# GpSimd's long subtractions split into two or four instructions each, in a two-layer decoder kernel

## The reference

```python
# layer 0: power attention with gates, 16 query heads on 8 key heads of 128
q, k, v = x @ Wq, x @ Wk, x @ Wv;  log_g = log_sigmoid(6.906768 + x @ Wg)
a = where(causal, (q k^T / sqrt(128)) ** 2 * exp(logG_t - logG_s), 0)
y = (a @ v / (sum(a) + 1e-6)) @ Wc + bc
# layer 0: causal attention on the context, 16 heads of 32, chunks of 256
# layer 0: experts: a router over 128, top 4, turned by amplitudes into 8 weights
#          for 8 gated bases of width 256, and two shared ones
...
# layer 1: multi-query attention with a memory, quantized cross attention,
#          a router over 8 small experts, top 2
```

## Time and profile before

| | |
|---|---|
| median of 3 runs | 2374.72 us (2372.3 to 2374.88) |
| profiled execution | 2378.91 us |
| its span | 2377.1 us |
| mean granted TensorE clock | 0.95 of full |
| PE busy | 2108.7 us, 89% |
| DVE busy | 1305.2 us, 55% |
| ACT busy | 1060.7 us, 45% |
| POOL busy | 796.7 us, 34%, 679 instructions |

### The profile page before, as it was taken

How to read it: one execution, slowest core, us unless ns; L and a number is a source line. 1 busy time by engine, 2 the same in 40 slices (tenths; PEclk the granted TensorE clock), 3 DMA queues, 4 the chain that set the end, 5 groups by cost and what they waited for, 6 DMA issues and landing times.

```text
span 2377.1 us, 37602 instructions
## 1 busy us (share of the span) xinstructions
PE 2108.7 (89%) x13655; PEld 1672.7 (70%) x13669; DVE 1305.2 (55%) x3333; ACT 1060.7 (45%) x2367; POOL 796.7 (34%) x679
## 2 busy tenths in 40 slices
PE   7899999898999978999999999968999778888764
PEld 6788888687878856877777888755555367666442
DVE  2554545544465456545456411356777676777555
ACT  3332332444444424445533312145666557777632
POOL 1743533333343222134431134254445231322100
PEclk9899999899999988999999999979999889999886
DMA  3311112011012012011110011033324210000001
GB/s 132 126 36 63 45 35 73 18 58 47 27 49 62 19 36 71 25 52 48 33 50 18 18 54 74 7 52 54 61 49 62 87 41 28 15 19 6 1 10 71
DMA packets 57878, 109.03 MB, mean 46 GB/s; under 512 B 7136, under 2 KB 35040, under 8 KB 54112
## 3 DMA queue, kind: packets, MB, share of 16 engines
q1 hardware_dynamic: 57696, 106.63, 15.4%
HBM read 86.10 MB, written 4.26 MB: 38 GB/s over the span
## 4 chain that ended last, share of the span: by engine, by line
PE 39%; DVE 10%; issue 7%; ACT 4%; POOL 2%; SPq 1%; DMA 1%; ACTq 0%; DVEq 0%; POOLq 0%
PE PS L1289 17%; PE PS L1880 3%; PE PS L1784 3%; PE PS L1305 2%; DVE st L191 2%; ACT xP L2545 2%; DVE aM L2020 1%; PE PS L1848 1%; PE PS L953 1%; PE PS L1868 1%; PE PS L965 1%; DVE PS L2667 1%; PE PS L1835 1%; ACT xN L240 1%; PE PS L1891 1%
## 5 line engine op out<-in xcount | busy, mean ns | idle before, releaser
L1289 PE MATMUL PS<-WH,bXH 128*128 128x512 f32 x640 | 258.7, 404 | 0.0
L1289 PE MATMUL PS<-WH,bXL 128*128 128x512 f32 x640 | 250.3, 391 | 0.0
L1289 PE MATMUL PS<-WL,bXH 128*128 128x512 f32 x640 | 250.2, 391 | 0.0
L2020 DVE TENSOR_REDUCE aM<-PS 128x4 f32<-128x1024 f32 x128 | 153.8, 1221 | 55.2 <-PE PS L1848 54.0
L384 PE MATMUL PS<-aXH,QKH 128*128 128x512 f32 x384 | 158.9, 414 | 14.6 <-ACT sq L597 8.4
L1586 POOL TENSOR_TENSOR mixed<-mixed,s 128x256 f32<-128x256 f32 x112 | 82.4, 739 | 245.5 <-DVE s L1487 245.3
L1590 POOL TENSOR_TENSOR WL<-sg,WH 128x2048 fp32r<-128x2048 f32 x20 | 92.1, 4604 | 186.5 <-ACT WH L1405 186.5
L384 PE MATMUL PS<-aXH,QKL 128*128 128x512 f32 x384 | 154.3, 402 | 0.0
L384 PE MATMUL PS<-aXL,QKH 128*128 128x512 f32 x384 | 154.0, 401 | 0.0
L1959 ACT ACTIVATE aPT<-PS 128x1024 f32<-128x1024 f32 x128 | 128.6, 1024 | 49.8 <-PE PS L1868 49.0
L684 DVE TENSOR_TENSOR qkL<-PS,qkH 128x512 fp32r<-128x512 f32 x96 | 65.9, 690 | 141.1 <-ACT qkH L561 141.0
(11 more groups left out here) (395 smaller groups left out, 6038.1 us busy)
## 6 DMA issues: line engine op xcount, KB each, us to landing
sg<-in_gu SPq DMA_DIRECT2D x16, 1024.0 KB, 4.8
gQK<-in_Wqk SPq DMA_DIRECT2D x16, 768.0 KB, 6.2
gC<-in_Wc SPq DMA_DIRECT2D x16, 512.0 KB, 7.0
lgB<-gate_sums SPq DMA_DIRECT2D x32, 256.0 KB, 4.6
aqs<-aQH SPq DMA_DIRECT2D x64, 128.0 KB, 4.1
xN<-in_xT SPq DMA_DIRECT2D x4, 1024.0 KB, 11.1
xN<-in_x SPq DMA_DIRECT2D x4, 1024.0 KB, 7.7
cst<-in_cT SPq DMA_DIRECT2D x8, 512.0 KB, 4.0
```

The source lines that it names most:

```text
L1289: mm = e.matmul(PS[:, b, :], x[:, kc, c:c + 128], y[:, kc, :], start=kc == 0 and n == 0, stop=kc == KC - 1 and n == 2)
L2020: e.tensor_reduce(M[j % 2][:, :, :].rearrange("x q (h c) -> x h q c", h=2)[:, :, :, i], PS[:, b:b + 2, :].rearrange("p h (q k) -> p h q k" ...
```

## The change

Six subtractions on POOL are each written as two or four instructions on the slices of their middle axis. The semaphore is raised by the last of them, and all waits stay where they were. The subtractions before the first step of `attention0` (L741, L744) are not changed. No other engine's sequence is changed.

```diff
-                    e.tensor_tensor(QKL[:, :, :], gQK[:, :, :], QKH[:, :, :].bitcast(F32),
-                                    ALU.subtract).then_inc(qk_lo.sem, 1)
+                    for kc in range(KC):
+                        last = e.tensor_tensor(QKL[:, kc, :], gQK[:, kc, :], QKH[:, kc, :].bitcast(F32), ALU.subtract)
+                    last.then_inc(qk_lo.sem, 1)
...
-                e.tensor_tensor(CL[:, :, :], gC[:, :, :], CH[:, :, :].bitcast(F32),
-                                ALU.subtract).then_inc(c_lo.sem, 1)
+                for h in (0, 1):
+                    last = e.tensor_tensor(CL[:, h, :], gC[:, h, :], CH[:, h, :].bitcast(F32), ALU.subtract)
+                last.then_inc(c_lo.sem, 1)
...
-                e.tensor_tensor(VL[:, :, 0:256], gV[:, :, 0:256], VH[:, :, 0:256].bitcast(F32),
-                                ALU.subtract).then_inc(v_lo.sem, 1)
+                for kc in range(KC):
+                    last = e.tensor_tensor(VL[:, kc, 0:256], gV[:, kc, 0:256], VH[:, kc, 0:256].bitcast(F32), ALU.subtract)
+                last.then_inc(v_lo.sem, 1)
...
-                    e.tensor_tensor(KL[:, c, :], cst[:, c, :], KH[:, c, :].bitcast(F32),
-                                    ALU.subtract).then_inc(k_lo.sem, 1)
+                    for k in (2 * i, 2 * i + 1):
+                        last_ = e.tensor_tensor(KL[:, k, :], cst[:, k, :], KH[:, k, :].bitcast(F32), ALU.subtract)
+                    last_.then_inc(k_lo.sem, 1)
...
-                e.tensor_tensor(WL[w % 2][:, :, :], sg[:, :, :], WH[w % 2][:, :, :].bitcast(F32),
-                                ALU.subtract).then_inc(w_lo.sem, 1)
+                for kc in range(KC):
+                    last_ = e.tensor_tensor(WL[w % 2][:, kc, :], sg[:, kc, :], WH[w % 2][:, kc, :].bitcast(F32), ALU.subtract)
+                last_.then_inc(w_lo.sem, 1)
...
-                e.tensor_tensor(DL[:, c:c + 2, :], dst[:, :, :], DH[:, c:c + 2, :].bitcast(F32),
-                                ALU.subtract).then_inc(d_lo.sem, 1)
+                for a in (0, 1):
+                    last_ = e.tensor_tensor(DL[:, c + a, :], dst[:, a, :], DH[:, c + a, :].bitcast(F32), ALU.subtract)
+                last_.then_inc(d_lo.sem, 1)
```

## The result

| | before | after |
|---|---|---|
| median | 2373.45 us (22 runs, 2366.63 to 2378.62) | 2369.71 us (22 runs, 2365.01 to 2376.52) |
| ratio | | 0.9984, 95% interval 0.9977 to 0.9992 |
| span of the profiled execution | 2377.1 us | 2368.8 us |
| POOL busy | 796.7 us in 679 | 822.0 us in 836 |

The changed kernel is 3.7 us faster (1.9 to 5.5 by the interval), less than the 0.2% that I called no change. I had forecast 2372.5 us and a gain of 2.25; 1.3 us of the distance to 2369.71 is the median of before, which was 2374.72 in the three runs that I had and is 2373.45 in 22. The two spans differ by 8.3 us, more than the medians.

What follows compares the result with a forecast made beforehand. PE, busy 89% of the span, was taken as the bound, so only places where it idles count: +2.2 + 0.8 + 0.5 - 1.05 - 2.3 - 2.4 + 0 = -2.25 us, from 2374.72 to 2372.5 us; range 2366 to 2379.

Steps and rivals of the forecast that it cites:

- What the pieces cost: On POOL: WL in four pieces takes 5.04 us for 4.60; over all 22.6 us more POOL time in 157 more instructions.
- Place 1: At 79 us, where PE waits for QKL: pieces and DVE instructions let in between make QKL end later, +2.2 us.
- Place 2: At 442 and 659 us: aT meets pieces of cKL, so PE's waits end later, +0.8 and +0.5 us.
- Place 3: At 859 us: L199, held beside CL, gets through after the first piece, -1.05 us.
- Place 4: At 1236 us: L219 held less by WL, -2.3 us; PE's clock then not falling, another -2.4 us.
- Place 5: At 1275 us: a chain of small dependent DVE instructions meets each WL piece in turn, so 0 us gained.
- small ones slip through: Rival: small dependent DVE instructions get in together between two pieces near 1275 us; sum -6.9 us, 2367.8 us, chance 0.13.
- slower: Rival: admissions cost more than they give at 79, 442 and 659 us, clock falls at 1243; +4.05 us, 2378.8 us, chance 0.17.
- No admission between pieces: Rival: POOL's pieces follow each other without letting DVE in, every hold longer; +2.2 us, 2376.9 us, chance 0.10.

Runs made afterwards that it cites:

- the kernel without WL: The change without its WL part (QKL, CL, VL, cKL, DL in pieces, the 20 WL whole), against before: 2375.34 us, ratio 1.0016.
- QKL alone: Only the 15 QKL in four pieces, all else as before; also called queries alone: 2375.76 us in one run.
- WL alone: Only the 20 WL in four pieces, everything else as before: 2364.3 us, ratio 0.9973.
- contexts alone: Only the 16 cKL in two pieces, all else as before: 2372.57 us in one run.
- the last kernel: Against before: WL 0 in four pieces, WL 10 and 11 whole behind waits, bias additions one step later: 2355.98 us, ratio 0.9938.
- waits and CL in two: Against before: WL 0, 10 and 11 whole but each behind one more wait on POOL, CL in two pieces: 2362.78 us, ratio 0.9957.
- WL in eight: Against before: WL in eight pieces of 128x256, CL in two, all else whole: 2361.75 us, ratio 0.996.
- three waits: Against before: all subtractions whole, WL 0, 10 and 11 each behind one more wait on POOL: 2360.31 us, ratio 0.9955.

## Why the prediction was right, and where not

- **What the pieces cost.** I had 5.04 us for WL in four and 22.6 us in all; the row at 1268.66 has 5.02, the page 25.3. I take the rest to be DVE let in between pieces, which I counted only at 79 us; it was not measured by itself.
- **Place 1: mechanism right, size too large.** I took +2.2 us. Counted between PE's instruction at 50 us and QKL's first, after and the kernel without WL have +1.6, QKL alone +1.1, WL alone 0. QKL began 0.6 us later, as I had said (0.65). What was too large is the price of DVE's admissions into QKL, 0.95 us, and the 0.2 added for a third: QKL grew by 1.06 us, 0.44 of it for the pieces, so the admissions cost 0.6. No row that I gave shows the 0.62 and 0.33 us per admission. That PE would start near 81.3 was wrong by 1 us, as the whole execution ran 1.4 us later by 50 us.
- **Place 2: right in sum, its cause only in part.** I put it all on cKL's and CL's pieces; at 442 us contexts alone give 0.3 us, CL in two without cKL 0.3 and queries alone 0.4, the longer QKL in front of them, which I had called free. Between 88 and 450 us after loses 0.75 us (I had 0.8), though with the two waits shared differently (1.82 and 0.87, since the lower clock now fell between them). At 660 us the wait grew by 0.4 us (I had 0.5). Behind it after and the kernel without WL both have a stretch at the lower clock (+1.5 us) that before hasn't; but so have WL alone and the last kernel, whose wait there is before's 1.27, and contexts alone has none. Whether the pieces cause it stays open. With it the kernel without WL sums to 1.6 + 0.75 + 0.4 + 1.5 - 1.05 = 3.2 us against 3.8 measured; without it to 1.7, at the edge of its interval (1.7 to 5.7).
- **Place 3: right at its wait.** -1.05 forecast; 4.49 to 3.41 us in every kernel with CL in two, and in no other. What follows I had not asked: in after, without WL and with waits and CL in two, PE needs another 1.1 us less between 874 and 891 us, where the lower clock lasts some 1.4 us less; with WL in eight the gain is lost again by 874 us. So the place is worth 0 to 2 us.
- **Place 4: right.** L219 in 4.28 us (about 4.3 forecast), wait down by 2.3, and the clock, the term I was least sure of, at 1.00: PE gains another 2.2 us over the next stretch, in all seven kernels in which this wait is 1.7 us or less. In the five profiles where it is about 4 us (3.98 to 4.15) the clock falls, which costs 2.2 us in two of them and 1.6 in three. But my reason for the term was weak, and that it held is luck in part: I chose between the wait of 1.66 us and that of 1.90, and behind this same wait at 442 us, again 1.90 and 1.88 us long, the clock is 1.00 in WL alone and in the last kernel. The length of one wait doesn't decide it.
- **Place 5: right.** Zero forecast, -0.2 measured, and the four holds of 1.2 us just as described. The rival in which small ones slip through is out. The Trainium skill (SBUF — State Buffer, section "Who interferes with whom") says that the port is held for a whole instruction; the 0.66 and 1.21 us for pieces of two sizes agree, and show that it comes free at each border, however short the gap. I had put no term in the sum for the clock behind this wait. It was 0.66 before and is 1.00 after, worth 1.6 us. All profiles with a wait of 2.9 us or more have the lower clock there and all with 1.02 us or less don't, but of the two with 2.73 us after has it not and WL alone has it.
- **The step that was missing: 900 us.** I looked for long DVE instructions beside long POOL ones and missed rL, held for 3.06 us in front of the longest wait of the first layer behind the start: -2.0, counted where PE goes on. Put into my sum with place 1 as measured, it gives -2.25 - 0.6 - 2.0 = -4.85, with 3.7 measured (1.9 to 5.5). The interval holds both this and my 2.25, so the time alone can't show that the term was missing; the trace does.

Of the rivals, "slower" needed all its terms: it had 4.4 us at 79 us, 2.5 at 442 and the clock falling at 1243, and the traces show 1.6, 0.75 and a clock at 1.00. "No admission between pieces" is refuted by the four holds of 1.2 us near 1270 and by rL and L219, which end before WL does.

## What to carry to other kernels

Where two engines exclude each other for the length of an instruction, cut the long one only where the held one is a single instruction in front of a wait of TensorE; against a chain of dependent small ones, pieces help only if they are more than the chain is long, and where TensorE waits for the long one itself, they cost time. A wait that starts the long instruction behind the held ones takes the whole hold away if its result isn't due soon: at 1243 and 1285 us PE's waits went altogether, where four pieces left 1.69 and 2.73 us and eight 0.6 and 1.02. But look at what the long one then falls on: at 900 us four pieces gave 2.0 us and the wait 0.6. By their times alone (10.7 us for three waits, 9.5 for WL in eight, 6.4 for WL in four, with intervals that overlap) the three aren't told apart. And look for such places along all of TensorE's waits, the longest first, as the one that I overlooked was the longest.

## What the runs showed of the hardware that I had not expected

- How long DVE work with one tensor as input is held follows POOL's piece: L219 (128x512, one input tile) took 4.78 us for its usual 0.54 beside a whole WL and 1.51 beside pieces of 1.3 us, and L199 (128x4) 1.85 us for 0.17 beside a whole WL that had begun before it.
- With the same code 238 us ran at the low clock level in one profile and 228 in the other. Two of these stretches (743 and 835 us) lie behind waits of PE of 1.05 and 0.87 us, a pair that all twelve profiles have at both places within 0.02 us; in five the clock falls behind it and in seven it doesn't. A clock term read from one profile is safe only where it repeats over several kernels, as at 1243 us.
